# Selective scan on one core: six of 32 steps take their drive from GpSimd and their decay from PSUM

## The reference, cut to what matters

```python
dt = softplus(einsum('blr,dr->bld', dt, dt_proj_w) + dt_proj_b)
A = -exp(A_log)                                  # 512 channels x 16 states
def step(s, inp):
    d, u_i, b_i, c_i = inp
    s = s * exp(d[..., None] * A) + (d * u_i)[..., None] * b_i[:, None, :]
    y = einsum('bdn,bn->bd', s, c_i)
    return (s, y)
```

## Time and profile before

| | before |
|---|---|
| median of 3 runs | 2707.36 us |
| the profiled execution | 2709.11 us, its span 2707.0 us |
| scan phase | about 0 to 1150 us of the span |
| busy over the whole span | PE 84%, DVE 73%, ACT 56%, POOL 48% |
| mean granted TensorE clock | 0.905 of full |

### The profile page before, as it was taken

One profiled execution on the slowest core, in us unless ns is written; L12 is line 12 of the kernel. 1 busy time (PEld: TensorE's weight loads), 2 busy tenths in 40 slices (PEclk: granted clock), 3 DMA queues, 4 the chain that ended last, 5 costly groups with the idle time before them and its releaser, 6 DMA issues. The chain is left out here.

```text
span 2707.0 us, 48178 instructions
## 1 busy us (share of the span) xinstructions
PE 2274.6 (84%) x16637; PEld 1559.6 (58%) x16637; DVE 1985.9 (73%) x4362; ACT 1510.2 (56%) x3353; POOL 1311.4 (48%) x1257
## 2 busy tenths in 40 slices
PE   4566978787878787879999988998987999899797
PEld 2345555555555555557777755655653665566555
DVE  4999999999999999536767646777775545556545
ACT  5666777777777775433333323544554666655522
POOL 1777777776777777423333323443564222221401
PEclk7768989898988898889999987998997999999899
DMA  5444334343434444110000034324303000000100
GB/s 162 124 130 122 132 119 133 120 134 118 133 121 132 122 133 133 56 47 28 1 1 1 9 76 73 63 53 68 70 5 104 16 18 21 17 18 17 48 14 9
DMA packets 134324, 196.22 MB, mean 72 GB/s; under 512 B 23953, under 2 KB 58898, under 8 KB 134082
## 3 DMA queue, kind: packets, MB, share of 16 engines
q1 hardware_dynamic: 132098, 190.24, 24.9%
q0 software_dynamic: 960, 2.62, 0.3%
q10 hardware_dynamic: 1024, 0.26, 0.1%
HBM read 153.95 MB, written 13.63 MB: 62 GB/s over the span
## 5 line engine op out<-in xcount | busy, mean ns | idle before, releaser
L403 POOL TENSOR_TENSOR ma_seen<-ma_state,ma_cs 128x1024 f32<-128x1024 f32 x256 | 603.6, 2362 | 320.6 <-DVE ma_state L984 319.0
L984 DVE TENSOR_TENSOR_SCAN ma_state<-ma_decay,ma_last,ma_drive 128x512 f32<-128x512 f32 x512 | 650.5, 1271 | 0.0
L971 DVE TENSOR_TENSOR ma_drive<-ma_weight,ma_bs 128x512 f32<-128x512 f32 x512 | 356.9, 697 | 30.5 <-DVE ma_state L984 1.9
L604 PE MATMUL ma_acc<-ident,ma_seen 128*128 128x128 f32 x2048 | 301.2, 299 | 88.2 <-POOL ma_seen L403 87.8
L604 PEld LDWEIGHTS ma_acc<-ident,ma_seen 128*128 128x128 f32 x2048 | 264.9, 156 | 177.6 <-POOL ma_seen L403 115.2
L830 ACT ACTIVATE ma_decay<-ma_dt,ma_a_neg 128x512 f32<-128x512 f32 x512 | 338.1, 709 | 0.0
L2110 DVE CUSTOM_DVE_ANT_0 sw_score<-sw_score,both_band 128x256 f32<-128x256 f32 (+1 forms) x512 | 197.7, 449 | 52.8 <-PE sw_score L1924 41.0
L2048 ACT ACTIVATE sw_prob<-sw_turned 128x512 f32<-128x512 f32 (+1 forms) x256 | 135.5, 581 | 180.7 <-PE sw_turned L1938 155.6
L104 POOL TENSOR_TENSOR moe_h_low<-both_V,light_wqkv 128x512 fp32r<-128x512 f32 x80 | 105.1, 1314 | 245.6 <-DVE light_wqkv L100 238.2
L1846 POOL TENSOR_SCALAR_AFFINE_SELECT sw_prob<-sw_prob 128x512 f32<-128x512 f32 x128 | 84.6, 661 | 214.3 <-ACT sw_prob L2048 214.3
L811 ACT ACTIVATE ma_last<-ma_state,ma_goes_on 128x2 f32<-128x2 f32 x255 | 74.1, 291 | 140.7 <-DVE ma_state L984 140.1
(11 more groups left out here) (550 smaller groups left out, 5601.6 us busy)
## 6 DMA issues: line engine op xcount, KB each, us to landing
ma_bs<-bc_rows SPq DMA_DIRECT2D x256, 256.0 KB, 3.2
ma_cs<-bc_rows SPq DMA_DIRECT2D x256, 256.0 KB, 3.3
both_wide<-both_kh SPq DMA_DIRECT2D x28, 192.0 KB, 4.2
both_wide<-both_qh SPq DMA_DIRECT2D x20, 256.0 KB, 4.5
x_rows<-X SPq DMA_DIRECT2D x1, 4096.0 KB
light_rows<-li_y SPq DMA_DIRECT2D x32, 128.0 KB, 1.7
out_dram<-li_o SPq DMA_DIRECT2D x32, 128.0 KB, 1.8
X<-in_L_attn_x_dram SPq DMA_DIRECT2D x1, 3584.0 KB, 13.8
```

The lines of the kernel that those rows point to most:

```text
L403: g.tensor_tensor(out=seen[n % RR][:, :, :], in0=state[n % SR][:, :, :], in1=each(cs[n % CR][:, :], 2), op=ALU.mult).then_inc(S["seen_full ...
L604: ins = t.matmul(accs(j, mm), seen[n % RR][:, mm, j * P:(j + 1) * P], K["ident"][:, :], is_transpose=True, start=False, stop=(last_ and j ...
L971: v.tensor_tensor(out=drive[mm][:, :], in0=weight[mm][:, :], in1=bs[n % CR][:, :], op=ALU.mult).then_inc(S["drive_done"], 1)
L984: v.tensor_tensor_scan(state[n % SR][:, mm, :], decay[s % DR][:, :], drive[mm][:, :], last[:, k, m:m + 1], ALU.mult, ALU.add).then_inc(S[" ...
```

## The change

In each group steps 7, 11, 14, 21, 27 and 29 are **pooled** (`on_pool`). For such a step:

- POOL makes both drives in one 128x1024 product, `wdt` times `bs`, into a new SBUF tile `pdrive` (`pool_drives`). It stands in POOL's list behind the weighing of three steps before. There is one such tile, so it waits until the scans of the pooled step before it are finished.
- DVE makes no drive; its scans read the decay from the PSUM bank `drive[mm]` and the drive from `pdrive`.
- ACT writes the step's two decays into the banks `drive[0]` and `drive[1]` (`bank_decay`), the first at the end of its fixed work for the step before, once the first scan of that step has released the bank, the second as its first work of the step itself, in front of everything else. They are no longer made two steps ahead.

To make room in SBUF `seen` has three buffers instead of four. POOL's `dt_weight` of the second half moves from step 6 to step 12, because steps 7, 11 and 14 still read the `wdt` of the first half. The counts that SP and ACT wait for skip the pooled steps. The core of the diff:

```diff
-DR, SR, RR, CR = 6, 4, 4, 3
+DR, SR, RR, CR = 6, 4, 3, 3
+POOLED = (7, 11, 14, 21, 27, 29)
...
+def on_pool(n):
+    return n % Q in POOLED
...
+def drives_before(n):
+    return 2 * (n - pooled_before(n))
...
+def slot_freed(n):
+    at = drives_before(n) // 2 - DR // 2
+    return 2 * DRIVEN[at] + 2 if at >= 0 else 0
...
+        pdrive = A.sb("pdrive", [P, 2, GN])
...
             def b_spread(n):
                 i, q = divmod(n, Q)
-                since(sp, "drive_done", 2 * (n - CR + 1))
+                if n >= CR and on_pool(n - CR):
+                    sp.wait_ge(S["pool_drive_done"], pooled_before(n - CR) + 1)
+                else:
+                    since(sp, "drive_done", drives_before(n - CR + 1))
...
+            def pool_drives(n):
+
+                if n >= Q * GROUPS or not on_pool(n):
+                    return
+                i, q = divmod(n, Q)
+                pool.wait_ge(b_in[n % CR], 16 * (n // CR + 1))
+                pool.wait_ge(S["wdt_done"], 2 * i + q // NS + 1)
+                since(pool, "scan_done", 2 * max((k + 1 for k in range(n) if on_pool(k)), default=0))
+                g.tensor_tensor(out=pdrive[:, :, :], in0=wdt[:, :, :], in1=each(bs[n % CR][:, :], 2), op=ALU.mult).then_inc(S["pool_drive_done"], 1)
...
                 for q in range(Q):
                     weigh(i, q)
+                    pool_drives(Q * i + q + 3)
...
-                    if q == 6:
+                    if q == 12:
                         dt_weight(i, 1)
...
             def decays(n):
...
+                if on_pool(n):
+                    return
                 act.wait_ge(S["dt_done"], 2 * i + h + 1)
-                since(act, "scan_done", 2 * n + 2 - DR)
...
+                since(act, "scan_done", slot_freed(n))
...
+            def bank_decay(n, mm):
...
+                since(act, "scan_done", 2 * n - 1 + mm)
+                a.activation(drive[mm][:, :], dt[:, m, :], ACT.Exp, scale=a_neg[:, m, k:k + 1]).then_inc(S["bank_decay_done"], 1)
...
                 for q in range(Q):
                     n = Q * i + q
+                    if on_pool(n):
+                        bank_decay(n, 1)
                     if n:
                         keeps(n - 1)
...
                     if n + 2 < Q * GROUPS:
                         decays(n + 2)
+                    if on_pool(n + 1):
+                        bank_decay(n + 1, 0)
...
+                if on_pool(n):
+                    if mm == 0:
+                        dve.wait_ge(S["pool_drive_done"], pooled_before(n) + 1)
+                    dve.wait_ge(S["bank_decay_done"], 2 * pooled_before(n) + mm + 1)
+                    keep, add = drive[mm][:, :], pdrive[:, mm, :]
```

33 lines of the change are left out of this document (23 added, 10 removed).

## The result

The changed kernel takes 2719.2 us (median of 20 runs) against 2700.5 us for the kernel before on the same chip (20 runs). The ratio is 1.0062, with a 95% interval of 1.0047 to 1.0077: 13 to 21 us slower. The profiled execution took 2715.9 us, its span 2714.2. One execution each of two later kernels was slow (over 3650 us) and is left out of their figures. The forecast was 2696; the rival called "slower" stood at 2717.

The account below looks back on a forecast made before the run. VectorE was taken to bound the scan phase, with in-order ScalarE often late. First group 3.7 plus last 8.5 less 1.5 in the middle groups gave 11 us off the 2707.4 median: 2696 us, 8-in-10 range 2666 to 2717.

Parts of the forecast that it names:

- slower: Rival: ScalarE as late at step 26 in every middle group as in the third; 10 us slower, 2717; chance 0.18.
- the term that it put at nothing: Whole kernel, after the rivals: the granted clock stays and nothing touches PE's, so no change from it.
- Steps 27 and 29: End of a middle group: late exponential, then six POOL products; the two cost 2.5 us instead of bringing 3.0.
- ScalarE also starts the group up to 1 us later: Start of a middle group: ScalarE's copies behind POOL's finishing of the rows come late, up to 1 us.
- What is removed: VectorE: two drives fewer per pooled step save 1.5 us, 73 us over 48 steps; ceiling 2634 us.
- The pooled scan and the exponential into PSUM: VectorE's scan with decay from PSUM, drive from SBUF: no change; ScalarE's exponential into PSUM: 0.66 us.
- First group and last group: First gains 3.7 us, only POOL binding; last 8.5, as ScalarE idles, POOL has no dt work, all six count.
- the 28.2 of the prediction: POOL's eleven products from weighing 24 on put the group's end 28.2 us after step 24's, against 27.5 before.
- POOL's single pdrive buffer, and the seen buffers: Step 29's product waits for step 27's end, six products follow, 14.0 us; supply of seen buffers counted as hidden.
- Steps 7 and 11: Middle groups: second exponential of 7 behind PE's block, ScalarE late at step 10; the pair put at -0.7 us.
- The sum: Six middle groups together about -1.5 us, first 3.7 and last 8.5 gained: 11 us off the median, 2696.
- The predicted signs of being wrong: Middle groups 4 us or more shorter, or waits standing at b rows or seen buffers, counted as hidden.

Follow-up runs that it names:

- three such steps: Steps 14, 17 and 21 pooled instead of the six, against the kernel before: 0.9862, 2667.2 us.
- one experiment: The changed kernel with POOL's products for steps 27 and 29 cut to two elements: 2702.2 us, 0.9974 of the kernel before.
- the pairs: Against the kernel before: steps 14 and 21 pooled, 0.9940; 7 and 11 added to these, 0.9919; 27 and 29 alone, 1.0049.

## Why the prediction was wrong

The forecast failed at the term that it put at nothing: "It changes nothing if the granted clock stays, and nothing here touches PE's." The lower clock stretched the block in front of step 24 from 3.60 to 5.30 us in the fifth to seventh groups, and the dt pairs at a group's start from 1.12 to 2.07 us. It so enlarged the two terms that hang on PE, "Steps 27 and 29" and "ScalarE also starts the group up to 1 us later". The six middle groups lost 22.5 us where about 1.5 were forecast; of the 21 more, 12 lie in steps 1 to 13 and nearly all the rest in 25 to 31. The clock's part is 5.1 us at the three slow blocks, as measured, and most of the 12 if a start at the lower clock costs 3.1 us here too, which is an estimate from the kernel with 14, 21, 27 and 29. Point by point:

- *What is removed*: right. Step 21 won 1.5: steps 20 and 21 last 3.10 and 3.26 us instead of 3.90 and 4.01. Step 14 won its 1.2, half of it in step 13 (3.74 against 4.34), half in itself (4.92 against 5.51), which is why the column 14-19 shows 0.6.
- *The pooled scan and the exponential into PSUM*: right, 1273 ns, and 65.3 us for 96 exponentials, 684 ns each and 0.61 from its start to that of the next instruction. The Trainium skill, "GPSIMD Engine Reference", "Specifications", names contention with POOL for VectorE instructions with two SBUF inputs or in a 2-port perf mode. The pooled scan has one large SBUF tensor, and the trace agrees that it isn't held up: POOL was busy 108 us more, and the scans are 2 ns longer.
- *First group and last group*: signs right, sizes 3.4 (3.7 forecast) and 4.0 (8.5). In the last, steps 25 to 31 won 2.8 and 7 and 11 little; the group starts with ScalarE late, which "all six count" left out.
- *Steps 27 and 29*: the mechanism right, and in the third and fourth groups nearly the size. I had ScalarE start 0.4 us later "by step 21's exponentials", at step 26 4.2 us behind VectorE; there it is 0.5 and 4.3, and 25 to 31 takes 30.5 us against some 29.9. In the fifth to seventh the block in front takes 1.7 us longer at the lower clock: ScalarE is 6.0 us late at step 26, on top of the 1.51 us that VectorE waits for step 26's decays, and 25 to 31 takes 32.2. From 20 to 31 the sixth group loses 3.3 us, where 1.0 was forecast. Moving two copies ahead took away both PE's wait and the slow block, and the stretch fell to 28.3, the 28.2 of the prediction.
- *POOL's single pdrive buffer, and the seen buffers*: the six products behind step 27's scan were right (14.0 us forecast, 13.9 measured). But the product waits only 0.48 us for that scan, because POOL has waited 1.94 and 4.67 us for PE's sums: a second chain of the same length, from the seen buffers, whose supply I had counted as hidden. With PE on time it is: with none pooled the loss is nil. Whether a fourth buffer would take that chain away was not tried; the first chain would still be there.
- *Steps 7 and 11*: forecast a loss of 0.7 a group; measured, 1 to 13 takes 3.4 us longer in the sixth group, of which most is the group's start: without 27 and 29 the same two steps lost about 0.7 (5.4 us over the phase), and in the groups of equal clock they add 1.2. I had put the late start at 1 us and ScalarE is about 4 us later at step 2, 1.9 of it the lower clock where that could be measured. The rest is POOL: its late end passes to the weights (ScalarE waits 3.10 us) and to the sums for which PE waits (3.52 and 2.06 us), and both meet ScalarE in its first three steps.
- *The sum*: by its own terms the six middle groups come to -2.0 us, not -1.5; that changes nothing.
- *The rivals*: "slower: the late wdt decides" named the place, and its size came out partly by luck. It asked for ScalarE as late at step 26 in every middle group as in the third (4.85 us); measured are 4.1 to 4.3 in the second to fourth and 6.0 in the others. It foretold 3.5 to 4 lost in each, 22 us; measured are 1.6, 0, 3.4, 5.4, 6.1 and 6.0, together 22.5, but 12 of them in steps 1 to 13, for which it had no extra loss, and the two ends won 7.4 us, not 12. Its chance of 0.18 was too low. What spoke for it, two groups out of six late already, was the slow block in just these two groups of the trace before (4.98 and 4.65 us), which the prediction did not use.

The predicted signs of being wrong, b rows or seen buffers as a cause of waits, are half there: 39 us of POOL's idle time before a weighing end on PE's sum (1.5 before the change).

## What to carry to other kernels

Making work early is what hides an in-order engine's lateness; where a change takes the margin away (here a decay two steps ahead became an exponential just in time), pool only the steps at which that engine is measured to be on time: three such steps gained 1.4%, six chosen by VectorE's saving lost 0.6%. Where repeats of the same code differ in a trace (here two groups of six), look for the row that differs before calling the state typical: it was a TensorE block at the lower clock, worth 1.7 us a group, where the added work itself was worth 0.5. Compare two kernels only by repeats with the same clock: 3.8 us by which one experiment seemed to shorten a stretch were 2.1 of its own and 1.7 of the clock. And test parts alone and together: the pairs' own effects (-21, +5.4, +12 us of phase) add to -4, all six gave +16.

## What the runs showed of the hardware

- A scan with decay from PSUM and drive from SBUF costs what the reverse costs (1273 and 1269 ns).
- PE's granted clock fell behind waits as short as these: after 3.52 and 2.06 us of idle time the windows show 0.71 and 0.50, and a pair of dt products takes 2.07 us instead of 1.12. It fell even after 6 us in which PE was busy for 5.91, with one wait of 1.23 behind them. The same waits also stood in front of blocks at full clock (2.23 us before 3.60 us of work in one group, before 5.30 in another), so from a wait alone these runs do not tell whether the clock falls.
- What it costs can be more than the wait: PE's wait in front of the block grew by 1.7 us (0.49 to 2.23) and a block at the lower clock takes another 1.7; 1.9 us of lateness from two dt pairs became a wait of 3.09 us on VectorE eleven steps later.
